# Reordering the steps of five engine programs in a pooled-attention and selective-scan kernel

## What is computed

```python
# layer 0: attention over a 2x2 max-pooled map
theta, phi, g = x @ w_theta, pool(x @ w_phi), pool(x @ w_g)
x = x + sigma * (softmax(theta @ phi.T) @ g @ w_o + b_o)
# layer 1: a selective scan (Mamba mixer) over the pixels in four orders
hs, gate = split(rmsnorm(x, w1) @ W_in.T)
hs = silu(causal_conv4(hs) + conv_b)
dt_r, B, C = split(hs @ W_x.T);  dt = softplus(dt_r @ W_dt.T + b_dt);  A = -exp(A_log)
state[n] = exp(dt*A[n]) * state[n] + dt * B[n] * hs      # along the pixels, n = 0..15
y = sum_n state[n] * C[n] + hs * Dp
out = rmsnorm(x + (y * silu(gate)) @ W_out.T)            # in each order
o = layernorm(mean of the four orders) 
```

## Time and profile before

| what | value |
|---|---|
| median of three runs | 966.35 us (964.02 to 968.66) |
| span of the profiled execution | 963.9 us |
| the profiled execution's own time | not listed apart from its span; the runs listed beside it took 964.02, 968.66 and 966.35 us |
| busy, of the span | PE 88%, DVE 87%, POOL 85%, ACT 61% |
| moved by DMA | 258.35 MB, 268 GB/s over the span |
| mean granted clock of PE | 0.951 of full speed |

### The profile page before, as it was taken

How to read it: one execution, slowest core, us unless ns; L and a number is a source line. 1 busy time by engine, 2 the same in 40 slices (tenths; PEclk the granted TensorE clock), 3 DMA queues, 4 the chain that set the end, 5 groups by cost and what they waited for, 6 DMA issues and landing times.

```text
span 963.9 us, 8874 instructions
## 1 busy us (share of the span) xinstructions
PE 846.2 (88%) x2178; PEld 363.3 (38%) x2178; DVE 839.9 (87%) x632; ACT 585.7 (61%) x798; POOL 819.0 (85%) x374
## 2 busy tenths in 40 slices
PE   5688989989898899989989898998989889898776
PEld 2233433334443334334343333333443333433322
DVE  2489999888999988998998999999899989889991
ACT  3575765848476583855758486574857657484331
POOL 0598997979989797997989799898989979798990
PEclk9799999989999998989999999999999999899997
DMA  1699688978778798778869788896988779689760
GB/s 46 222 295 305 244 274 285 315 261 281 262 291 303 260 313 293 260 252 288 314 255 318 266 282 258 306 312 253 309 283 280 262 285 325 244 301 302 263 247 3
DMA packets 78051, 258.35 MB, mean 268 GB/s; under 512 B 13104, under 2 KB 15408, under 8 KB 78000
## 3 DMA queue, kind: packets, MB, share of 16 engines
q1 hardware_dynamic: 78000, 257.79, 77.4%
HBM read 254.60 MB, written 3.15 MB: 267 GB/s over the span
## 4 chain that ended last, share of the span: by engine, by line
POOL 51%; DMA 17%; issue 17%; PE 6%; DVE 5%; ACT 3%; SPq 1%; POOLq 1%; DVEq 0%; ACTq 0%
POOL inp L881 31%; POOL state L887 17%; DMA b_all<-bc_dram 14%; DMA c_all<-bc_dram 3%; POOL du L871 3%; DVE ps_x L1031 2%; PE ps_y L546 1%; DVE state L1031 1%; PE ps_w L459 1%; DVE state L1038 1%; ACT ps_x L730 1%; PE ps_x L531 1%; SPq L308 0%; PE ps_w L507 0%; POOL step L873 0%
## 5 line engine op out<-in xcount | busy, mean ns | idle before, releaser
L881 POOL TENSOR_TENSOR inp<-du,b_all 128x1024 f32<-128x1024 f32 x224 | 521.9, 2354 | 4.9 <-DMA b_all<-bc_dram 4.0
L546 PE MATMUL ps_y<-state,packed 128*128 128x512 f32 x1024 | 495.6, 623 | 19.5 <-POOL state L887 19.5
L1031 DVE TENSOR_TENSOR_SCAN ps_x<-ps_x,inp 128x1024 f32<-128x1024 f32 x144 | 329.3, 2287 | 42.5 <-ACT ps_x L730 29.8
L887 POOL TENSOR_TENSOR state<-state,c_all 128x1024 f32<-128x1024 f32 x112 | 262.0, 2351 | 87.0 <-DVE state L1024 49.4
L730 ACT ACTIVATE ps_x<-step,a_neg 128x1024 f32<-128x1024 f32 x224 | 247.1, 1112 | 137.7 <-DVE state L1038 101.0
L546 PEld LDWEIGHTS ps_y<-state,packed 128*128 128x128 f32 x1024 | 194.2, 197 | 267.5 <-issue 213.0
L1038 DVE TENSOR_TENSOR state<-ps_x,c_all 128x1024 f32<-128x1024 f32 x144 | 175.9, 1222 | 4.2 <-issue 0.7
L1031 DVE TENSOR_TENSOR_SCAN state<-ps_x,inp 128x1024 f32<-128x1024 f32 x80 | 179.1, 2272 | 0.0
L531 PE MATMUL ps_x<-u,w_b_wide 128*128 128x512 f32 x128 | 68.0, 656 | 9.4 <-DVE state L1038 9.3
L1024 DVE TENSOR_TENSOR_SCAN state<-decay,ps_x 128x1024 f32<-128x1024 f32 x32 | 73.0, 2281 | 0.5
L459 PE MATMUL ps_w<-xpad,w_conv 128*128 128x512 f32 x128 | 61.6, 605 | 3.3 <-ACT xpad L692 3.3
(11 more groups left out here) (116 smaller groups left out, 676.4 us busy)
## 6 DMA issues: line engine op xcount, KB each, us to landing
c_all<-bc_dram SPq DMA_DIRECT2D x256, 512.0 KB, 6.8
b_all<-bc_dram SPq DMA_DIRECT2D x224, 512.0 KB, 6.0
xt<-in_x_t SPq DMA_DIRECT2D x32, 64.0 KB, 3.3
bc_dram<-bc_rows SPq DMA_DIRECT2D x32, 64.0 KB, 3.2
out<-ofin SPq DMA_DIRECT2D x16, 64.0 KB, 1.6
packed<-in_packed SPq DMA_DIRECT2D x1, 635.0 KB, 4.2
packed<-in_packed SPq DMA_DIRECT2D x1, 129.0 KB, 2.1
w_qkv<-in_w_qkv SPq DMA_DIRECT2D x1, 64.0 KB, 2.2
```

Of the source, the lines that this page charges most:

```text
L546: last = mm(ps_y[:, HALF * half:HALF * (half + 1)], ident, state[n % H_RING][:, HALF * half:HALF * (half + 1)], start=(n == 0), stop=(n == ...
L881: tt(inp[i % IN_RING][:, :], du[b.buf][:, :], b_all[i % B_RING][:, :], ALU.mult).then_inc(pool_inputs, 1)
L887: tt(state[n % H_RING][:, :], state[n % H_RING][:, :], c_all[n % C_RING][:, :], ALU.mult).then_inc(pool_products, 1)
L1031: v.tensor_tensor_scan(held if KIND[n] == "P" else x, x, inp[i % IN_RING][:, :], 0.0, ALU.mult, ALU.add).then_inc(scans, 1)
```

## The change

The step functions, their waits and all instructions stay as they are. Only the order of the calls in the `prologue`, `steps` and `finish` functions of SP, PE, ACT, POOL and DVE changes. On POOL the first product of the coming image goes behind its input 2, and inputs 3, 5, 6, 7 and product 3 are counted to the image before. On DVE products 5 and 6 come behind scans 5 and 6, products 7 and 8 behind scans 7 and 8; pooling and row maximum are earlier and the softmax division is behind scan 12; product 15 of an image opens the next call (so it stands in `finish` for the last). On ACT decays 5 and 8 and the decays 2 and 9 go ahead of the activations that stood before them. On PE the attention steps of the later image, and the spread for state 0, are further ahead. SP's queue follows these orders. The diff, with the lines between cut out (the hunks are SP, PE, ACT twice, POOL, DVE):

```diff
@@ -340,55 +340,55 @@
...
     load_b(first, 3)
-    load_b(first, 5)
     load_c(first, 0)
...
     load_c(first, 2)
+    load_b(first, 5)
     load_b(first, 6)
-    load_c(first, 3)
+    load_b(first, 7)
 
 def finish(j):
...
 def steps(b, done, coming, later):
-    load_b(b, 7)
+    load_c(b, 3)
+    load_c(b, 4)
+    load_c(b, 5)
     load_b(b, 8)
+    load_b(b, 9)
+    load_b(b, 10)
+    load_c(b, 6)
     if later:
         load_x(later)
-    load_c(b, 4)
-    load_b(b, 9)
-    load_c(b, 5)
-    load_c(b, 6)
-    load_b(b, 10)
     load_c(b, 7)
     load_b(b, 11)
+    load_b(b, 12)
     load_c(b, 8)
-    load_b(b, 12)
-    load_b(b, 13)
     load_c(b, 9)
     load_c(b, 10)
+    load_b(b, 13)
+    if coming:
+        store_bc(coming)
     load_b(b, 14)
-    load_b(b, 15)
-    if coming:
-        store_bc(coming)
     load_c(b, 11)
     load_c(b, 12)
+    load_b(b, 15)
     load_c(b, 13)
     load_c(b, 14)
+    load_c(b, 15)
     if coming:
         load_b(coming, 1)
-    if done:
-        store_out(done)
-    load_c(b, 15)
-    if coming:
         load_b(coming, 2)
         load_b(coming, 3)
-        load_b(coming, 5)
         load_c(coming, 0)
...
         load_c(coming, 2)
+        load_b(coming, 5)
         load_b(coming, 6)
-        load_c(coming, 3)
+    if done:
+        store_out(done)
+    if coming:
+        load_b(coming, 7)
 
@@ -601,21 +601,23 @@
...
     sum_state(b, 1)
-    sum_state(b, 2)
     if coming:
...
         conv(coming, 1)
-    sum_state(b, 3)
+    sum_state(b, 2)
     if coming:
...
         step_proj(coming, 0)
+    sum_state(b, 3)
     sum_state(b, 4)
...
         bc_proj(coming)
+    if later:
+        qkv(later)
     sum_state(b, 5)
...
     if later:
-        qkv(later)
+        scores(later)
     skip(b, 0)
@@ -624,18 +626,16 @@
...
     sum_state(b, 10)
+    if later:
+        attn_turn(later)
+    if done:
+        out_final(done)
     sum_state(b, 11)
     if later:
-        scores(later)
-    if done:
-        out_final(done)
-    if later:
-        attn_turn(later)
+        attn_out(later)
+    if coming:
+        spread_b(coming, 0)
     sum_state(b, 12)
-    if coming:
-        spread_b(coming, 0)
-    if later:
-        attn_out(later)
 
@@ -790,10 +790,10 @@
...
     softplus(first)
-    sb_decay(first, 0)
     theta_copy(second)
...
     attn_copy(second)
+    sb_decay(first, 0)
 
 def finish(j):
@@ -807,49 +807,47 @@
...
     ps_decay(b, 1)
+    ps_decay(b, 2)
     if coming:
         rms_inverse(coming)
-    ps_decay(b, 2)
+        pad(coming)
+    if done:
+        hid_squares(done)
     ps_decay(b, 3)
     if done:
-        hid_squares(done)
-    if coming:
-        pad(coming)
-    if done:
         hid_inverse(done)
+    ps_decay(b, 5)
     if coming:
...
         out_squares(done)
-    ps_decay(b, 5)
     ps_decay(b, 6)
...
     ps_decay(b, 7)
+    ps_decay(b, 8)
     if coming:
         softplus(coming)
-    ps_decay(b, 8)
+        bc_copy(coming)
     ps_decay(b, 9)
-    if coming:
-        bc_copy(coming)
-    ps_decay(b, 10)
-    if coming:
-        sb_decay(coming, 0)
     if later:
         theta_copy(later)
+    ps_decay(b, 10)
     ps_decay(b, 11)
+    if done:
+        out_inverse(done)
     ps_decay(b, 12)
-    if done:
-        out_inverse(done)
+    if later:
+        softmax_exp(later)
     ps_decay(b, 13)
...
     if later:
-        softmax_exp(later)
+        attn_copy(later)
+    if coming:
+        sb_decay(coming, 0)
     if done:
         out_copy(done)
-    if later:
-        attn_copy(later)
     ps_decay(b, 15)
@@ -893,35 +891,40 @@
...
     scan_input(first, 2)
+    scan_input(first, 3)
+    scan_input(first, 5)
+    scan_input(first, 6)
+    scan_input(first, 7)
+    product(first, 3)
 
 def finish(j):
...
 def steps(b, done, coming, later):
-    scan_input(b, 3)
-    scan_input(b, 5)
-    scan_input(b, 6)
-    scan_input(b, 7)
+    product(b, 4)
     scan_input(b, 8)
-    product(b, 3)
-    product(b, 4)
     scan_input(b, 9)
     scan_input(b, 10)
+    scan_input(b, 11)
     if coming:
         scan_weight(coming)
-    scan_input(b, 11)
     scan_input(b, 12)
+    scan_input(b, 13)
     product(b, 9)
     product(b, 10)
-    scan_input(b, 13)
     scan_input(b, 14)
+    scan_input(b, 15)
     product(b, 12)
-    scan_input(b, 15)
     product(b, 13)
...
         scan_input(coming, 1)
+        scan_input(coming, 2)
         product(coming, 0)
-        scan_input(coming, 2)
+        scan_input(coming, 3)
+        scan_input(coming, 5)
+        scan_input(coming, 6)
+        scan_input(coming, 7)
+        product(coming, 3)
 
@@ -1075,52 +1078,55 @@
...
 def finish(j):
+    product(j, 15)
     gated(j)
...
 def steps(b, done, coming, later):
+    if done:
+        product(done, 15)
     scan(b, 0)
...
         gated(done)
+    product(b, 1)
     if coming:
         rms(coming)
-    product(b, 1)
     scan(b, 2)
...
     scan(b, 3)
+    scan_input(b, 4)
     if done:
         hid_norm(done)
-    scan_input(b, 4)
     scan(b, 4)
     scan(b, 5)
+    scan(b, 6)
     product(b, 5)
-    scan(b, 6)
     product(b, 6)
     scan(b, 7)
+    scan(b, 8)
     product(b, 7)
-    scan(b, 8)
     product(b, 8)
+    if later:
+        pooling(later)
     scan(b, 9)
...
     if later:
-        pooling(later)
+        row_max(later)
     product(b, 11)
     scan(b, 12)
+    if later:
+        attn_norm(later)
     scan(b, 13)
-    if later:
-        row_max(later)
-        attn_norm(later)
     scan(b, 14)
...
         scan_input(coming, 0)
-    product(b, 15)
 
```

More of the change, by code:

```diff
@@ L353, in steps @@
             def steps(b, done, coming, later):
-                load_b(b, 7)
+                load_c(b, 3)
+                load_c(b, 4)
+                load_c(b, 5)
                 load_b(b, 8)
+                load_b(b, 9)
+                load_b(b, 10)
+                load_c(b, 6)
                 if later:
                     load_x(later)
-                load_c(b, 4)
-                load_b(b, 9)
-                load_c(b, 5)
-                load_c(b, 6)
-                load_b(b, 10)
                 load_c(b, 7)
                 load_b(b, 11)
+                load_b(b, 12)
                 load_c(b, 8)
-                load_b(b, 12)
-                load_b(b, 13)
                 load_c(b, 9)
                 load_c(b, 10)
-                load_b(b, 14)
-                load_b(b, 15)
+                load_b(b, 13)
                 if coming:
                     store_bc(coming)
+                load_b(b, 14)
                 load_c(b, 11)
                 load_c(b, 12)
+                load_b(b, 15)
                 load_c(b, 13)
                 load_c(b, 14)
+                load_c(b, 15)
                 if coming:
                     load_b(coming, 1)
-                if done:
-                    store_out(done)
-                load_c(b, 15)
-                if coming:
                     load_b(coming, 2)
                     load_b(coming, 3)
-                    load_b(coming, 5)
                     load_c(coming, 0)
@@ L626, in steps @@
                 sum_state(b, 10)
+                if later:
+                    attn_turn(later)
+                if done:
+                    out_final(done)
                 sum_state(b, 11)
                 if later:
-                    scores(later)
-                if done:
-                    out_final(done)
-                if later:
-                    attn_turn(later)
-                sum_state(b, 12)
+                    attn_out(later)
                 if coming:
                     spread_b(coming, 0)
-                if later:
-                    attn_out(later)
+                sum_state(b, 12)
             program(pe, prologue, steps, finish)
@@ L829, in steps @@
                 ps_decay(b, 7)
+                ps_decay(b, 8)
                 if coming:
                     softplus(coming)
-                ps_decay(b, 8)
+                    bc_copy(coming)
                 ps_decay(b, 9)
-                if coming:
-                    bc_copy(coming)
-                ps_decay(b, 10)
-                if coming:
-                    sb_decay(coming, 0)
                 if later:
                     theta_copy(later)
+                ps_decay(b, 10)
                 ps_decay(b, 11)
-                ps_decay(b, 12)
                 if done:
                     out_inverse(done)
+                ps_decay(b, 12)
+                if later:
+                    softmax_exp(later)
                 ps_decay(b, 13)
```

## The result

The changed kernel takes 951.64 us in the median (949.11 to 952.36, four runs), the kernel before 965.18 (963.15 to 968.66). The ratio is 0.9848, 95% interval 0.982 to 0.9877: faster, by 1.5%. The forecast was 909 us with a range of 896 to 934. The direction was right; three quarters of the expected gain did not come. Of the prediction's rivals, the fall of PE's clock once an image (945 us, chance 0.10) lies nearest.

The account below looks back on a forecast made before the run. It took waits in a loop between DVE and POOL as the bound. Cutting the period from 56.75 to 53.1 us gives 51.1, plus 2.9 and 3.4 at the ends: span 906.5, forecast 909 us, range 896 to 934.

Parts of the forecast that it names:

- the fall of PE's clock once an image: Rival: PE's clock still falls once an image, costing 2.6 us a period on a loop without slack; 945 us, chance 0.10.
- item 5: DVE runs two scans, then two products (5,6 and 7,8): saves 0.5 us a period, costs 0.2 at scan 7.
- Item 7: Check of PE's loop through gating, product 6 and decay 8: 53.2 us, within 0.4 of the other; period taken as 53.1.
- item 6: Small waits the new order adds across the engines: 1.2 us a period in sum, bounds 0 and 3.
- Item 1: On ACT, decay 5 ahead of SiLU 0, decay 8 ahead of softplus, decays 2 and 9 likewise: saves 2.3 us a period.
- Item 2: On DVE, softmax division one scan later, so product 11 and scan 12 cover the exponential: saves 1.0 us a period.
- Item 3: On PE, state 0's spread ahead of sum 12, attention steps ahead of sum 11, at full clock: most of 0.8 us.
- Item 4: On POOL, product 0 behind input 2: its wait shrinks from 5.1 to about 1 us a period; product 4 waits 0.7.
- Item 8: Transfers: DMA share rises from 0.82 to 0.88, with room; C0 and C11 arrive in time, C11 being tight.
- Item 9: Ends of the run: 2.9 us gained in the prologue and 3.4 us in the last image.
- The rule against it: Skill's rule for ACT table loads: a 1.38 us drain on top, 2.66 a switch, where the trace shows 1.30.
- the better case: Rival: every cover holds, 52.1 us a period; 895 us, chance 0.06.

Follow-up runs that it names:

- e6: Changed kernel plus four matrix products an image (D times u added and taken off) in PE's gap ahead of the B and C projection: 921.51 us, ratio 0.9541.
- e1: Changed kernel plus one call asking for the exponential's table right behind the gate's SiLU, ahead of decay 7: 905.14 us, ratio 0.941.
- e8: Kernel before with only decay 5 moved ahead of SiLU 0 and decay 8 ahead of softplus: 975.71 us, ratio 1.0118.
- e12: e1 with the row maximum moved back right ahead of the softmax division, both behind scan 12: 929.37 us, ratio 0.9616.
- e4: Changed kernel with the coming image's product 0 ahead of input 2 on POOL again: 951.95 us, ratio 0.9873.
- e2: Changed kernel with scan and product in turn again for states 5 to 8 on DVE: 903.98 us, ratio 0.9374.
- e9: e1 with SP's list of transfers as it was before the change: 917.77 us, ratio 0.9495.
- e10: e8 with the changed kernel's list of transfers on SP and nothing else: 955.56 us, ratio 0.9879.

## Why the prediction was wrong

The step that failed is the end of item 5, "The price: scan 7 stands behind products 5 and 6 with only 1.14 us to cover decay 7's 1.12 and the signals. I take 0.2." It covered decay 7's 1.12 us and left out the 1.28 of the table load in front of it, as if the load were done while ACT waits for product 5. It is not; the load waits too, and scan 7 waited 1.46 where the sum has 0.2. Item 7 has the same gap: its loop goes from product 6 straight to decay 8. I had the loads in the text (as many before and after, and a rule on their price) and never asked where each one stands to the wait beside it. The earlier trace rows show a load with no idle time ahead of it, which says only that its wait was already over there.

The second step that failed hangs on the first. The rival "the clock still falls once an image" was held unlikely because the idle pieces of PE were computed as 0.9, 0.6 and 0.8 us. With softplus later by the load the one ahead of the projection was 2.14, and the clock fell. The price was put at 2.6 us a period, from the slow turn and spread of the kernel before, and measured at 2.1 (e6) at the projection. Together, 1.28 and 2.1 a period are the difference between 951.6 and the 905.1 of e1.

With the load out of the way the period comes out as forecast, though not every term of it does:

- Period: 53.1 forecast, 52.83 in e1. DVE's floor 51.6, measured 51.5 (721.36 / 14); DVE's idle time 1.2 forecast, 1.3 measured (739.59 less 721.36, by 14). The time, 909 forecast, 905 in e1. In part that is luck: scan 6 waits 0.40 where item 6 has 0.15, and the waits given to the gating and to decay 15, 0.3 together, do not show.
- Item 1 (decays ahead of SiLU and softplus): the waits at scans 5 and 8 went as said, but e8 shows that this alone is a loss of 1.2% in the old order. As a term of a sum, a gain of 2.3, it was wrong there; what it gives beside the other orders was not measured alone.
- Item 2: 1.0 forecast; e12 gives 1.7 a period, as scan 13's wait for its decay goes with it.
- Item 3: PE no longer waits for the division, and the spread's wait on DVE fell from 10.8 to 4.6 us, 0.44 a period where "most of" 0.8, less the 0.2 of item 6, was forecast. Right in kind, a little short in size.
- Item 4: e4 shows that the new place of product 0 recovers nothing in the changed kernel. Before the change 46.2 of the 71.4 us that make the 5.1 are for scan 0, so the wait reads as a sign of DVE's lateness; no run takes it apart. In e1 the "about 1" forecast for it did not come: in the image below product 0 starts 0.1 us after the input ahead of it ends. The wait that e1's fourteen periods do show is product 4's, 1.0 a period where item 4 has 0.7. Products 0 and 4 in one image, then POOL's waits for these scans in the window:

```profile
465.31 2.34 POOL L886 TENSOR_TENSOR state<-state,c_all 128x1024 f32<-128x1024 f32 x1
...
480.32 2.35 POOL L886 TENSOR_TENSOR state<-state,c_all 128x1024 f32<-128x1024 f32 x1 [1.10 <-DVE state L1028]
```

```profile
POOL state L886 <- DVE state L1028: 14.5, 14, 1.1
```

- Item 5: its gain of 0.5 a period is what put the load in the way. With scan and product in turn (e2) the same kernel is 48 us faster.
- Item 7: two loops within 0.4 us of each other and no slack. The runs bear it out: 1.3 us on one ACT wait and the slow products behind it came through in full, 3.3 a period.
- Item 8: no transfer is waited for in the changed kernel's window but for 3.3 us on POOL. Right, yet it was told as a check and not as a part that gains, which e9 and e10 show it to be.
- Item 9: the first image gained 1.4 us (2.9 forecast, 2.4 in e1, where scan 0 of image 1 starts at 92.8), the last 2.8 (3.4): 889.64 to the end of the span was 74.3, 879.08 to the end is 71.4.
- The rule against it: in e1 the load starts at 485.03 and the decay at 486.34, 1.31 us start to start, and 1.29 in both switches shown of the changed kernel. The Trainium skill (ScalarE: Activation LUTs, section What ACT_TABLE_LOAD costs) adds a drain to each switch. No drain shows in these rows.
- The range was said to take in the better case (895) and the lower bound of the sum (892), but its lower end is 896. This changes nothing for 951.6.

## What to carry to other kernels

When a step that needs another activation table also waits for a semaphore, look in the profile at whether the load starts before or only after that wait ends; if a predecessor can be late, ask for the table explicitly behind the last use of the old one. In a schedule where three engines are each near 90% busy, do not sum the waits that an edit takes away: find the loop, and test each cover with the loads and the queue of transfers in it. And a wait on PE is worth its length only while the clock holds; cheap work put into a gap can be worth more than the gap.

## What the runs showed of the chip that I had not expected

Adding 1.7 us of matrix products to each image made the kernel 30 us faster (e6). The granted clock stayed at 1.00 with idle pieces of 0.96 and 0.85 us around the projection (e1) and with 0.42 and 0.85 (e6), and fell with 2.14 and 0.85 (changed kernel), with the same work behind. The length of one piece does not decide it alone: in e8, whose work around the projection is in another order, the clock stayed at 1.00 from 238 to 254 us around a piece of 2.50 us, and had fallen behind one of 2.22 us at 526.74.
